# Small attention and third attention of a four-layer transformer chain: squares, root chains, key banks and transfers rearranged

## The chip, the cores and the metric

One Trainium2 chip, one core. The kernel is one program on that core. The metric is its device time in microseconds (us). Five engines have their own instruction streams and meet through semaphores: TensorE (PE), VectorE (DVE), ScalarE (ACT), GpSimd (POOL) and SyncE (SP, which issues the DMAs). SBUF is the large on-chip memory, PSUM the eight 2 KB-per-partition banks into which TensorE writes.

## What is computed

x is [8, 128, 512] in fp32 (8 batches of 128 tokens of 512 values). Eight stages follow, each of the form x = x + stage(layernorm(x)): attention with its own keys and bias (stage 0), a SiLU feed-forward with low-rank parts (1), the small attention (2), a feed-forward that picks one of 32 weights (3), the third attention, with normalised queries and keys (4), a mixture of low-rank experts (5), the last attention (6) and a GELU feed-forward (7). What bears on the change:

```python
# every stage: layernorm over the 512 values, mean and variance of each token

# small attention (stage 2): 8 batches x 4 patches of 128 positions, 8 heads of 8 values
scores = einsum('bhdi,bhdj->bhij', qh, kh) / sqrt(8)
scores = where(mask > 0, scores, -1e9);  attn = softmax(scores)
o = gelu(einsum('bhij,bhdj->bhdi', attn, vh))
out = (Wo @ o + bo) * mask

# third attention (stage 4): 32 query heads, 8 key/value heads, 128 values each
q = rmsnorm(q, q_norm_w);  k = rmsnorm(repeat(k, 4), k_norm_w)   # 1/sqrt(mean(square) + 1e-5)
attn = softmax(q @ k^T / sqrt(128) + mask);  out = (attn @ v) @ Wo
```

## The kernel before

**General.** Everything stays in SBUF: x (8 tiles of 128 x 512), the layernormed x transposed (xnT) and the context (ctxT), each as a high and a low part, so that an fp32 product is three matmul passes (`pe_matmuls`, L386). PSUM has eight banks: `proj[0..1]`, `score[0..1]`, `turn`, `heado`, `outp[0..1]`. The order on each engine is written out by hand; each engine runs its queue in that order, and a waiting instruction holds all behind it.

**Layernorm statistics.** Most stages get the mean from a sum that the last addition of the stage before delivers as it adds (`dve_add_sum`, L491), and the variance from squares with an accumulator on ScalarE (`act_ln_deviations`, L495). Stages 0 and 2 (`BN_STAGES`, L453) use two DVE instructions instead, `bn_stats` and `bn_aggr` (`dve_ln_stats`, L455, instructions at L457 and L459). Then `dve_ln_rstd` (L461) computes 1/sqrt for four batches at a time: one instruction for the argument (L466 or L468), two of bit tricks and three Newton steps of three instructions each (`dve_rsqrt`, L422, instructions L426 to L436), every one waiting for the one before; outside `BN_STAGES` one more for the shift (`recentre`, L473). Its arrays `nw_v`, `nw_t` and `rstd` lie in SBUF.

**Small attention** (L1733 to L2103). It follows the last output product of the SiLU feed-forward, whose eight additions to x are L1593. Head of the stage on DVE (`l1_dve`, from L2057): add and statistics for batches 0 to 3, adds 4 and 5, first root chain, normalised x of batches 0 and 1 (`norm`, L1988), masked keys of batch 0 (L1995), adds 6 and 7 with the other statistics, low part of the queries (L2000), values of batch 0 (L2009), last statistics, the second root chain, and only then the loop over 64 units (8 batches x 8). A unit is 4 heads of one patch: PE forms the scores (L1852) from a block-diagonal key tile, DVE takes the row maximum (L2016), ACT the exponentials (L1945), PE turns them (L1860) and multiplies with the values (L1872). Work for the next batch is strewn among the units of the present one (`extras`). POOL (`l1_pool`) makes the low part of the keys (L1799), the live mask of the *next* batch (`mask_keys`, L1789), and then the eight block-diagonal key tiles of the present batch (L1808), which also need rows of the mask that SP brings (`rows`, L1754, four small DMAs a batch). SP (`l1_sp`) waits for the last product of the feed-forward and issues one mask row for the tail (L1764), eight mask tiles for the tail (`tail`, L1745), and then `rows(0)`.

**Third attention** (L853 to L1310, `A.normed`). Eight groups g of one key/value head and four query heads j; a step (g, j) on PE is: scores of the next head, the projections that are `needed`, pieces of an output product (`out_at`), for each half a turn of the probabilities (L937) and a product with the values into `heado` (L950), then turns. For the root mean squares, raw queries and (at j = 1) the raw keys of the next group are turned by PE into `proj[0]` and `proj[1]` (`turn_for_sums`, L872, L883) and ScalarE squares and sums them from there (`sum_squares`, L1052, L1060). At j = 1 the queries come first, then the keys, into the same two banks. DVE makes the roots (`rms`, L1199, instructions L1207 and L426 to L436) with work values in `heado` (queries) or `score[0]` (keys). At j = 2 of every group but the last (`spreads`) DVE runs the keys' root chain, adds two output products to x (L1233), makes eight diagonals (`make_diagonals`, L1214), and PE spreads the roots over `turn` (L892). Group 0 and the last group are written out, groups 1 to 6 are a loop. PE's projection in a step waits for the squares of the last turns into `proj` (`last_sums`, L788).

## Time and profile before

| | us |
|---|---|
| median of 3 runs | 3076.47 (3075.88 to 3076.72) |
| profiled execution | 3081.03 |
| its span, first to last instruction | 3079.2 |
| PE busy | 2936.5 (95%) |
| DVE busy | 1723.2 (56%) |
| ACT busy | 1113.6 (36%) |
| POOL busy | 986.4 (32%) |
| small attention, first last-addition to next feed-forward | about 1108 to 1319 |
| third attention | about 1539 to 2216 |

Busy time is the sum of instructions; a PE at 95% still idles 143 us in the span, and it is there, at the joints between stages and in short waits inside a group, that a change of order can act. The chain of work that ended last runs through PE for 88% of the span and through DVE for 7%.

### The profile page before, as it was taken

What the parts mean: (1) busy time and instruction counts of PE and PEld (TensorE: products, weight loads), DVE (VectorE), ACT (ScalarE), POOL (GpSimd) and SP (SyncE); (2) the same over time, 40 slices, a digit from 0 to 9 for tenths busy, and PEclk for the clock granted to TensorE, in tenths of its full rate; (3) what the DMA queues carried; (4) which work ended last, traced back from release to release, by engine and by line L of the source; (5) the groups of instructions that cost most, each with busy time, mean ns of one, the idle gap of its engine ahead of it and who ended that gap; (6) DMA issues with size and microseconds to landing.
All of it is one profiled execution on the core that took longest, in us unless ns stands there. A gap on an engine that the chain in (4) does not pass through costs nothing.

```text
span 3079.2 us, 47940 instructions
## 1 busy us (share of the span) xinstructions
PE 2936.5 (95%) x16224; PEld 2492.1 (81%) x16224; DVE 1723.2 (56%) x3514; ACT 1113.6 (36%) x3615; POOL 986.4 (32%) x836
## 2 busy tenths in 40 slices
PE   7999999999999989899989999999889999999899
PEld 6888888888878857688778888888768888888787
DVE  6544444454552268777666666666644445444644
ACT  4222223222242237732344444444423333333432
POOL 4333333333222246433333222332213333332221
PEclk9999999999999999899999999999999999999999
DMA  3111101111111010011111001110011111110111
GB/s 120 41 48 40 47 30 47 39 40 47 37 49 48 27 42 29 27 35 41 32 39 32 28 27 34 34 34 17 25 41 41 39 37 34 34 34 21 45 45 48
DMA packets 68564, 119.74 MB, mean 39 GB/s; under 512 B 8681, under 2 KB 14185, under 8 KB 68065
## 3 DMA queue, kind: packets, MB, share of 16 engines
q1 hardware_dynamic: 68450, 118.26, 12.3%
q8 instruction: 67, 1.10, 0.1%
q14 instruction: 47, 0.39, 0.0%
HBM read 116.06 MB, written 2.10 MB: 38 GB/s over the span
## 4 chain that ended last, share of the span: by engine, by line
PE 88%; DVE 7%; ACT 3%; issue 2%; DMA 0%; POOL 0%; SPq 0%; DVEq 0%; ACTq 0%; POOLq 0%
PE proj L390 40%; PE outp L390 23%; PE heado L950 6%; PE score L917 5%; PE turn L937 3%; PE score L390 2%; PE outp L1872 1%; PE score L1454 1%; PE proj L406 1%; ACT sq L1060 1%; PE proj L883 1%; PE heado L1872 1%; DVE x L1691 0%; PE proj L1837 0%; PE turn L869 0%
## 5 line engine op out<-in xcount | busy, mean ns | idle before, releaser
L390 PE MATMUL outp<-w_out,acts 128*128 128x512 f32 x3288 | 840.7, 400 | 25.9 <-DVE x L1233 12.6
L390 PE MATMUL proj<-xnT,w_in 128*128 128x512 f32 x3192 | 758.0, 393 | 4.5 <-issue 2.3
L390 PEld LDWEIGHTS outp<-w_out,acts 128*128 128x128 f32 x3288 | 595.2, 188 | 154.0 <-DVE x L1233 16.4
L390 PEld LDWEIGHTS proj<-xnT,w_in 128*128 128x128 f32 x3192 | 593.6, 188 | 130.1 <-issue 2.7
L390 PE MATMUL proj<-ctxT,w_kv 128*128 128x512 f32 x1536 | 367.4, 395 | 18.7 <-POOL w_kv L697 18.7
L695 POOL TENSOR_TENSOR w_out<-ring,consts 128x512 fp32r<-128x512 f32 x96 | 101.9, 1062 | 830.0 <-PE outp L390 830.0
L390 PEld LDWEIGHTS proj<-ctxT,w_kv 128*128 128x128 f32 x1536 | 288.3, 190 | 77.8 <-issue 18.6
L1233 DVE TENSOR_TENSOR x<-x,outp 128x512 f32<-128x512 f32 x360 | 244.8, 685 | 186.7 <-PE outp L390 184.9
L1015 DVE COPY big<-proj 128x512 f32<-128x512 f32 x136 | 93.7, 689 | 348.7 <-PE proj L390 346.2
L1012 ACT ACTIVATE big<-proj 128x512 f32<-128x512 f32 x136 | 81.4, 599 | 496.9 <-PE proj L390 490.4
L695 POOL TENSOR_TENSOR w_kv<-ring,consts 128x512 fp32r<-128x512 f32 x93 | 97.0, 1043 | 459.6 <-DMA ring<-in_L_wk 439.3
L1093 ACT ACTIVATE acts<-heado 128x512 fp32r<-128x512 f32 x192 | 114.7, 597 | 325.1 <-PE heado L950 325.1
L1257 DVE TENSOR_TENSOR acts<-heado,acts 128x512 fp32r<-128x512 f32 x192 | 132.8, 692 | 174.1 <-ACT acts L1093 174.1
L950 PEld LDWEIGHTS heado<-ptbuf,big 128*128 128x128 f32 x1536 | 201.5, 192 | 30.9 <-ACT ptbuf L1091 15.6
L950 PE MATMUL heado<-ptbuf,big 128*128 128x128 f32 x1536 | 205.1, 277 | 12.3 <-ACT ptbuf L1091 6.9
L1091 ACT ACTIVATE ptbuf<-turn 128x512 f32<-128x512 f32 x192 | 114.3, 595 | 269.1 <-PE turn L937 268.8
L917 PEld LDWEIGHTS score<-big 128*128 128x128 f32 x1536 | 183.2, 192 | 8.9 <-issue 4.4
L917 PE MATMUL score<-big 128*128 128x128 f32 x1536 | 187.3, 275 | 3.0 <-issue 1.7
L390 PE MATMUL proj<-w_kv,ctxT 128*128 128x256 f32 x1536 | 183.4, 280 | 1.6 <-DVE big L1015 1.6
L390 PEld LDWEIGHTS proj<-w_kv,ctxT 128*128 128x128 f32 x1536 | 182.1, 188 | 3.1 <-DVE big L1015 1.9
L1593 DVE TENSOR_TENSOR x<-x,outp 128x512 f32<-128x512 f32 x160 | 109.7, 686 | 97.4 <-PE outp L390 97.0
L695 POOL TENSOR_TENSOR w_in<-ring,consts 128x512 fp32r<-128x512 f32 x96 | 106.6, 1111 | 166.1 <-PE proj L390 87.8
(303 smaller groups left out, 4129.3 us busy)
## 6 DMA issues: line engine op xcount, KB each, us to landing
ring<-in_L_wq SPq DMA_DIRECT2D x96, 256.0 KB, 2.7
ring<-in_L_wo SPq DMA_DIRECT2D x96, 256.0 KB, 2.6
ring<-in_F_in SPq DMA_DIRECT2D x52, 256.0 KB, 2.6
ring<-in_L_wk SPq DMA_DIRECT2D x48, 256.0 KB, 2.7
ring<-in_L_wv SPq DMA_DIRECT2D x48, 256.0 KB, 3.2
ring<-in_F_out SPq DMA_DIRECT2D x41, 256.0 KB, 2.6
x<-in_x SPq DMA_DIRECT2D x2, 1024.0 KB, 8.4
big<-in_ctxT SPq DMA_DIRECT2D x4, 512.0 KB, 8.0
```

Source lines behind the costliest of these rows:

```text
L390: mm = pe.matmul(bank_ap, w_ap(a, c), rhs(b, c), start=first and c == 0 and n == 0, stop=last and c == chunks - 1 and n == len(PASSES) - 1)
L695: pool.tensor_tensor(dst[:, slot, 0, :], ring[:, r, :], zeros512, ALU.add).then_inc(m["high_w"], 1)
L917: mm = pe.matmul(score[half][:, b * P:(b + 1) * P], qT[:, t], kT[:, t], start=True, stop=True)
L937: mm = pe.transpose(turn[:, b * P:(b + 1) * P], probs[j % 2][:, half, b * P:(b + 1) * P], ident)
L950: mm = pe.matmul(heado[:, b * P:(b + 1) * P], v_pair[:, n, j % 2, :] if A.own_kv else v[:, n * S:(n + 1) * S], ptbuf[:, half, b * P:(b + 1 ...
L1012: return engine.activation(dst, src, ACT.Copy)
L1015: return engine.tensor_copy(dst, src)
L1091: act.activation(ptbuf[:, half, :], turn[:, :], ACT.Copy).then_inc(m["tfree"], 1)
L1093: act.activation(acts[:, j, 0, half * HALF:(half + 1) * HALF], heado[:, :], ACT.Copy)\
L1233: dve.tensor_tensor(x[:, b, :], x[:, b, :], outp[b % 2][:, :], ALU.add).then_inc(m["added"], 1)
L1257: dve.tensor_tensor(acts[:, j, 1, cols], heado[:, :], acts[:, j, 0, cols].bitcast(F32), ALU.subtract)\
L1593: dve.tensor_tensor(x[:, b, :], x[:, b, :], outp[b % 2][:, :], ALU.add).then_inc(m["added"], 1)
```

## The change

Small attention: stage 2 leaves `BN_STAGES`; the feed-forward's last additions deliver sums; ScalarE squares; `norm` uses `rstd` and `recentre`. The second root chain goes from before the unit loop to behind unit 3, with its argument and work values in `outp[1]`. SP issues `rows(0)` ahead of the nine mask transfers. POOL makes the live mask of batch 1 after the second key tile, not before the first. Third attention: the raw keys at j = 1 are turned into `turn` and `heado`, with waits for those banks in place of the wait for the squares in `proj`; the query roots of that step work in `proj[1]`, so PE's next projection into `proj[1]` waits for the roots; the first addition of step j = 2 goes into the middle of the keys' root chain and the second behind it.

```diff
@@ dve_rsqrt
+        def dve_rsqrt(dve, y, arg, tmp, shifted, newton, calls, between=None):
...
             for n in range(3):
+                if n == 1 and between:
+                    between()
                 dve.tensor_tensor(tmp, y, arg, ALU.mult).then_inc(newton, 1)
...
-        BN_STAGES = [0, 2]
+        BN_STAGES = [0]
...
+        def dve_ln_rstd(dve, n, half, arg=None, work=None):
             cols = slice(half * BH, half * BH + BH)
+            arg, work = (nw_v[:, cols], nw_t[:, cols]) if arg is None else (arg, work)
...
+        def sum_banks(j, what):
+            return (turn, heado) if j == 1 and what == "k" else proj
...
         def last_sums(g, j):
-            return 5 * g + (2, 3, 4 if is_last_group(g) else 5, 6)[j]
+            return 5 * g + (2, 3, 4, 6)[j]
@@ project_head
                     m.wait(pe, "squared", 2 * squares + (half + 1))
+                if roots is not None and half == 1:
+                    m.wait(pe, "newton", 9 * roots)
@@ turn_for_sums
-                    m.wait(pe, "squared", 2 * c + (half - 1))
+                    if unit_left is None:
+                        m.wait(pe, "squared", 2 * c + (half - 1))
+                    elif half == 1:
+                        m.wait(pe, "low", unit_left + 1)
...
-                        mm = pe.transpose(proj[half][:, b * P:(b + 1) * P], src[:, t], ident)
+                        mm = pe.transpose(banks[half][:, b * P:(b + 1) * P], src[:, t], ident)
@@ attention_pe, step
-                    project(*new, squares=last_sums(g, j) if n == 0 else None)
+                    project(*new, squares=last_sums(g, j) if n == 0 else None,
+                            roots=newton_calls(g, j) if A.normed and j == 2 and n == 0 else None)
...
+                    if spreads(A, g, j) and half == 0:
+                        m.wait(pe, "squared", 2 * rms_call(g + 1, 0, "k") + 2)
                     m.wait(pe, "pready", unit(g, j, half) + 1)
@@ attention_dve, step
                 if spreads(A, g, j):
-                    rms(g + 1, 0, "k")
-                add_at(0)
+                    rms(g + 1, 0, "k", between=lambda: add(2 * out_g + pair, 0))
+                    add(2 * out_g + pair, 1)
+                else:
+                    add_at(0)
...
-                        rms(*n, lows=2 * (GH * g + j) + 2)
+                        rms(*n, lows=2 * (GH * g + j) + 2, scratch=proj[1] if j == 1 and not is_last_group(g) else None)
@@ ffn_dve, last_add
-                add(p, b, summed=A is F1)
+                add(p, b, summed=A is not F3)
@@ l1_sp
                     F0.events.wait(sp, "outfull", B * ((F0.chunks + 1) // 2))
+                    rows(0)
...
-                if b:
+                if b > 1:
                     rows(b - 1)
@@ l1_pool
-                if b + 1 < B:
+                if 0 < b < B - 1:
                     mask_keys(b + 1)
...
                 for u in range(UNITS):
+                    if b == 0 and u == 2:
+                        mask_keys(1)
@@ l1_act
+            for b in range(BH + 2):
+                deviations(b)
             F0.events.wait(act, "outfull", B * ((F0.chunks + 1) // 2))
...
+            for b in range(BH + 2, B):
+                deviations(b)
+            act.wait_ge(ln_moments, 8 * 2 + B)
             for u in range(UNITS * B):
@@ l1_dve
-            for b in range(BH):
+            for b in range(BH + 2):
                 add_of(b)
-                dve_ln_stats(dve, 2, b)
-            add_of(BH)
-            add_of(BH + 1)
             dve_ln_rstd(dve, 2, 0)
             norm(0)
             norm(1)
-            dve_ln_stats(dve, 2, BH)
             for s in range(2):
                 take_keys(0, s)
             add_of(BH + 2)
-            dve_ln_stats(dve, 2, BH + 1)
-            dve_ln_stats(dve, 2, BH + 2)
-            add_of(BH + 3)
             for s in range(2):
                 low_of_queries(0, s)
+            add_of(BH + 3)
             take_values(0)
-            dve_ln_stats(dve, 2, BH + 3)
-            dve_ln_rstd(dve, 2, 1)
             for u in range(UNITS * B):
                 maxima(u)
                 if u >= 2 and u % 2:
                     take_turned(u - 2)
                 extras(u // UNITS, u % UNITS)
+                if u == 3:
+                    dve_ln_rstd(dve, 2, 1, outp[1][:, 0:BH], outp[1][:, BH:B])
```

## Rows read from the trace of the kernel before

**Rows 1.** The page: busy time, share of the span, instructions of PE.

```profile
PE 2936.5 (95%) x16224; PEld 2492.1 (81%) x16224; DVE 1723.2 (56%) x3514; ACT 1113.6 (36%) x3615; POOL 986.4 (32%) x836
```

**Rows 2.** Windows: start:end, length, busy (instructions) per engine, granted clock, DMA, GB/s.

```profile
1128.00:1138.00 10.00, 4.59 (x6) 1.62 (x6) 9.55 (x16) 1.06 (x4) 7.18 (x8) 0.67 0.14 48
...
1158.00:1178.00 20.00, 18.43 (x126) 14.57 (x125) 17.61 (x28) 14.26 (x44) 12.24 (x11) 1.00 0.09 27
```

**Rows 3.** Timeline, DVE, small attention's head: start us, us, instruction [idle before, releaser].

```profile
1114.31 1.39 DVE L1593 TENSOR_TENSOR x<-x,outp 128x512 f32<-128x512 f32 x2
...
1128.18 1.04 DVE L466 TENSOR_SCALAR nw_v<-moments 128x4 f32<-128x4 f32 x1
...
1136.21 0.69 DVE L2016 TENSOR_REDUCE negmax<-score 128x4 f32<-128x512 f32 x1
...
1145.08 0.69 DVE L2016 TENSOR_REDUCE negmax<-score 128x4 f32<-128x512 f32 x1 [0.44 <-PE score L1852]
```

**Rows 4.** Timeline, PE, the same stretch.

```profile
1108.59 0.39 PE L1440 MATMUL outp<-low_b,low_in 96*128 96x512 f32 x1
...
1109.71 0.39 PE L1440 MATMUL outp<-low_b,low_in 96*128 96x512 f32 x1
...
1118.81 1.93 PE L1832 MATMUL proj<-sq,wk 128*96 128x512 f32 x4 [1.66 <-DVE sq L1988]
...
1128.46 0.77 PE L1852 MATMUL score<-stacks 98*128 98x512 f32 x1 [1.77 <-POOL stacks L1808]
...
1138.22 0.77 PE L1852 MATMUL score<-stacks 98*128 98x512 f32 x1 [5.18 <-ACT pbuf L1945]
```

**Rows 5.** Timeline, POOL, the same stretch.

```profile
1124.10 1.48 POOL L1789 TENSOR_SCALAR brow<-ring 96x512 f32<-96x512 f32 x1
1127.16 8.02 POOL L1808 TENSOR_TENSOR stacks<-spare,consts 98x512 fp32r<-98x512 f32 x8 [1.58 <-DMA spare<-ring]
```

**Rows 6.** Timeline, SP's DMA issues, the same stretch.

```profile
1117.19 0.24 SPq L1764 DMA_DIRECT2D big<-in_mask  x1
...
1122.62 2.48 SPq L1754 DMA_DIRECT2D spare<-ring  x4
```

**Rows 7.** Timeline, ACT: a table load in this head; another, with what follows.

```profile
1123.42 1.28 ACT L1945 ACT_TABLE_LOAD   x1
...
1283.04 1.28 ACT L1978 ACT_TABLE_LOAD   x1
1284.34 1.95 ACT L1978 ACTIVATE big<-big,vecs 64x512 f32<-64x512 f32 x3
```

**Rows 8.** Timeline, PE, third attention, j = 1 to j = 2 of one group.

```profile
1764.32 0.66 PE L883 MATMUL proj<-consts,spare 128*128 128x128 f32 x4 [0.85 <-ACT sq L1060]
1765.35 0.66 PE L883 MATMUL proj<-consts,spare 128*128 128x128 f32 x4 [0.37 <-ACT sq L1060]
...
1777.44 1.67 PE L390 MATMUL outp<-w_out,acts 128*128 128x512 f32 x6 [0.86 <-DVE x L1233]
...
1781.67 1.05 PE L950 MATMUL heado<-ptbuf,big 128*128 128x128 f32 x8
```

**Rows 9.** Timeline, DVE, the same group.

```profile
1763.27 0.69 DVE L1257 TENSOR_TENSOR acts<-heado,acts 128x512 fp32r<-128x512 f32 x1 [0.83 <-ACT acts L1093]
...
1766.20 0.16 DVE L1207 TENSOR_SCALAR heado<-sumsq 128x8 f32<-128x8 f32 x1
...
1773.45 0.69 DVE L1015 COPY big<-proj 128x512 f32<-128x512 f32 x1 [1.08 <-PE proj L390]
...
1776.70 1.29 DVE L1233 TENSOR_TENSOR x<-x,outp 128x512 f32<-128x512 f32 x2 [0.23 <-DVE rk L436]
1777.90 1.65 DVE L1214 TENSOR_SCALAR spare<-consts,rk 128x128 f32<-128x128 f32 x8
...
1780.67 0.69 DVE L1257 TENSOR_TENSOR acts<-heado,acts 128x512 fp32r<-128x512 f32 x1 [0.52 <-ACT acts L1093]
```

**Rows 10.** Timeline, POOL, the same group.

```profile
1765.81 1.60 POOL L697 TENSOR_TENSOR w_in<-ring,w_in 128x512 fp32r<-128x512 f32 x1
```

More of the change, by code:

```diff
@@ L459, in dve_ln_stats @@
             dve.bn_aggr(moments[:, b, :], stats[:, b, :]).then_inc(ln_moments, 1)
-        def dve_ln_rstd(dve, n, half):
+        def dve_ln_rstd(dve, n, half, arg=None, work=None):
             cols = slice(half * BH, half * BH + BH)
+            arg, work = (nw_v[:, cols], nw_t[:, cols]) if arg is None else (arg, work)
             dve.wait_ge(ln_moments, 8 * n + half * BH + BH)
             if n in BN_STAGES:
-                dve.tensor_scalar(nw_v[:, cols], moments[:, cols, 1], EPS, None, ALU.add).then_inc(ln_rstd, 1)
+                dve.tensor_scalar(arg, moments[:, cols, 1], EPS, None, ALU.add).then_inc(ln_rstd, 1)
             else:
-                dve.tensor_scalar(nw_v[:, cols], sqdev[:, cols], 1.0 / D ** 3, EPS, ALU.mult, ALU.add).then_inc(ln_rstd, 1)
+                dve.tensor_scalar(arg, sqdev[:, cols], 1.0 / D ** 3, EPS, ALU.mult, ALU.add).then_inc(ln_rstd, 1)
             dve.wait_ge(ln_rstd, 2 * n + half + 1)
-            dve_rsqrt(dve, rstd[:, cols], nw_v[:, cols], nw_t[:, cols], ln_shifted, ln_newton, ln_calls[0])
+            dve_rsqrt(dve, rstd[:, cols], arg, work, ln_shifted, ln_newton, ln_calls[0])
             ln_calls[0] += 1
@@ L476, in centred @@
         def centred(n, half):
-            return 7 + 2 * (ln_no(n) - 1) + half + 1
+            return 7 + 2 * (n - 1) + half + 1
         NORMED_DVE = (4, 6)
@@ L830, in project_values, with project_head @@
                 mm.then_inc(m["pfull", half], 1)
-        def project_head(pe, A, g, j, what, squares=None, halves=(0, 1)):
+        def project_head(pe, A, g, j, what, squares=None, roots=None, halves=(0, 1)):
             m = A.events
@@ L855, in attention_pe @@
             unit = lambda g, j, half: 2 * (GH * g + j) + half
-            project = lambda g, j, what, squares=None: project_head(pe, A, g, j, what, squares)
+            project = lambda g, j, what, squares=None, roots=None: project_head(pe, A, g, j, what, squares, roots)
             def use_turn(n):
@@ L870, in turn_values, with turn_for_sums @@
                 mm.then_inc(m["tfull"], 1)
-            def turn_for_sums(g, j, what, taken):
+            def turn_for_sums(g, j, what, taken, banks=proj, unit_left=None):
                 c = rms_call(g, j, what)
@@ L957, in step @@
                 for new in turned_for_sums(A, g, j):
-                    turn_for_sums(*new, taken=needed(A, g, j)[-1])
+                    banks = sum_banks(j, new[2])
+                    turn_for_sums(*new, taken=needed(A, g, j)[-1], banks=banks,
+                                  unit_left=None if banks is proj else unit(g, j, 1))
                 if spreads(A, g, j):
@@ L1050, in attention_act, with sum_squares @@
             m = A.events
-            def sum_squares(g, j, what):
+            def sum_squares(g, j, what, banks=proj):
                 c = rms_call(g, j, what)
@@ L1059, in sum_squares @@
                         n = half * BH + b
-                        a = act.activation(sq[:, n * P:(n + 1) * P], proj[half][:, b * P:(b + 1) * P], ACT.Square,
+                        a = act.activation(sq[:, n * P:(n + 1) * P], banks[half][:, b * P:(b + 1) * P], ACT.Square,
                                            accum_out=sumsq[:, n:n + 1])
@@ L1097, in step @@
                 for new in turned_for_sums(A, g, j):
-                    sum_squares(*new)
+                    sum_squares(*new, banks=sum_banks(j, new[2]))
             def group(g):
@@ L1197, in normalise, with rms @@
                    .then_inc(m["pready"], 1)
-            def rms(g, j, what, lows=0):
+            def rms(g, j, what, lows=0, scratch=None, between=None):
                 m.wait(dve, "low", lows)
@@ L1204, in rms @@
                 m.wait(dve, "squared", 2 * c + 2)
-                scratch = score[0] if what == "k" else heado
+                scratch = scratch or (score[0] if what == "k" else heado)
                 mean, work = scratch[:, 0:B], scratch[:, B:2 * B]
@@ L1208, in rms @@
                 m.wait(dve, "meaned", c + 1)
-                dve_rsqrt(dve, dst[:, :], mean, work, m["shifted"], m["newton"], c)
+                dve_rsqrt(dve, dst[:, :], mean, work, m["shifted"], m["newton"], c, between)
             def make_diagonals():
@@ L1927, in l1_act, with deviations @@
             act.wait_ge(m["w_made"], 3)
+            def deviations(b):
+                F0.events.wait(act, "added", B * ((F0.chunks - 1) // 2) + b + 1)
+                act_ln_deviations(act, 2, b)
             def high_of_keys(b, s):
@@ L1987, in norm @@
                 wait(dve, m["q_full"], 2 * b - 2)
-                dve.tensor_scalar(xn1[b % 2], x[:, b, :], moments[:, b, 0:1], rstd[:, b:b + 1], ALU.subtract, ALU.mult)\
+                dve.wait_ge(ln_rms, centred(2, b // BH))
+                dve.tensor_scalar(xn1[b % 2], x[:, b, :], rstd[:, b:b + 1], recentre[:, b:b + 1], ALU.mult, ALU.add)\
                    .then_inc(m["normed"], 1)
```

3 lines of the change are left out of this document (1 added, 2 removed).

## The prediction

> **What bounds the kernel now.** I read the page first: PE is busy for 95% of the span [rows 1], so an edit pays where PE idles, or where PE runs at its lower clock, and nowhere else. Then the list of waits and PE's timeline in the two stages that the diff touches, and for every PE gap the timelines of the engines behind it.
>
> In the small attention's head PE all but stops. From 1128 to 1138 us it is busy 4.59 of 10 us, at a mean granted clock of 0.67 (one level is 2.4 GHz, the other, half of it, 1.2 GHz), while DVE is busy 9.55 us [rows 2]. The reader is to see why: the first scores are there at 1128.46 [rows 4], but DVE takes their maximum only at 1136.21, because the second root chain stands ahead of it from 1128.18 [rows 3]. That chain is 12 tiny instructions in 8.0 us, the first of 1.04 us; beside it POOL makes key tiles, eight in 8.02 us [rows 5]. In the third attention the same chain of 12 takes 2.4 us: from the end of the copy at 1773.45 + 0.6 to the add at 1776.70, less 0.23 of wait [rows 9], so 0.20 us each. Once the units run, PE is busy 18.43 of 20 us at full clock [rows 2]: a later start is never made up, and an earlier one is kept.
>
> In the third attention the gaps come once in each of seven groups (all but the last): 0.85 and 0.37 us ahead of the turned keys, which wait for ScalarE to empty `proj`, and 0.86 us ahead of an output product that waits for DVE's addition [rows 8]. They sum to 2.1 us of modelled idle time; from start to start the rows lose up to 2.4.
>
> **Small attention, step by step.** *Additions and statistics.* Six additions, four statistics and the chain stand ahead of the first norm. They end at 1114.31 + 1.39 = 1115.7 [rows 3]. Without the statistics PE sets the pace: two products in a row close 1.12 us apart [rows 4], an addition takes 0.7 [rows 3]. Product 2 closes at 1110.1, its addition begins at 1110.2, three more at 1.1 bring the sixth to 1113.5 and its end to 1114.2: 1.4 us earlier. The read of the accumulator that a summing add brings has 0.4 us of room in each step, so I cost it at nothing; without that room it would add under 0.1 us a step by my guess from the 0.16 to 0.2 us of the smallest instructions [rows 9], at most 0.6 in all. The chain gets one instruction more (`recentre`, 0.2). ScalarE, idle there, squares the first four batches beside it. Norm, PE's key projection (1118.81, released by the norm [rows 4]) and all behind it come 1.2 us earlier.
>
> *Rows first.* SP issues the row transfers at 1122.62, 5.4 us after its wait ended at 1117.19 [rows 6], and POOL starts the key tiles at 1127.16, having idled 1.58 us for them [rows 5]. Put first, they are issued over 2.5 us from about 1115.7 and land before 1121; nothing waits for them. What is late next is POOL's own queue: the low part of the keys ends where the mask begins, 1124.10 [rows 5], now 1122.9. The nine mask transfers move 2.5 us back in SP's queue; their reader is the stage's tail, over 100 us later. `ctx_tok` of batch 2 is queued behind them, and it needs values of batch 1, later still.
>
> *Live mask of batch 1.* It goes behind two key tiles. So POOL does tiles 0 and 1 (2.0 us) until 1124.9, the mask (1.5) until 1126.4, tile 2. DVE's masked keys of batch 1 (unit 0's extra) wait for that mask, and the maximum of unit 1 is queued behind them: about 1.5 us of DVE wait, which I count. From a tile's start to its scores is 1.3 us (1127.16 to 1128.46 [rows 4, 5]). Unit 2's scores, at 1138.22 before [rows 4], come at 1126.4 + 1.3 = 1127.7: **10.5 us earlier**.
>
> *Table load.* The load for the exponentials ran at 1123.42, long before the first of them [rows 7]. Squares of batches 6 and 7 now stand ahead of it; the last ends near 1124.5, the load 1.3 later at 1125.8, the first exponentials at 1127.0. That is under the 1127.7 that POOL sets, so it costs nothing. The Trainium skill (ScalarE: Activation LUTs, What ACT_TABLE_LOAD costs) speaks against this: it counts a drain of some 1.4 us on top of the load, 2.7 in all, which would push unit 2 to about 1128.4 and cost 0.7 us. The trace does not agree: 1.30 us from a load's start to the next instruction's [rows 7].
>
> *The late chain.* 13 instructions, behind unit 3. At 0.20 us each they hold DVE 2.6 us; DVE idled 0.44 there before the maximum of unit 4 at 1145.08 [rows 3]. Behind it wait low queries, then PE's value projection, then every later unit: 2.2 us lost on the path. POOL is multiplying beside it. With work values in SBUF each could cost 1.0 as in the 8.0 us above; with them in PSUM, the chain at 1766.20 ran in 0.2 steps (first instruction 0.16 us [rows 9]) beside a POOL instruction of 1.60 us [rows 10]. Only `recentre` still reads two SBUF arrays: up to 0.8 more. I take 2.4, near the row that has PSUM. The Trainium skill (GPSIMD Engine Reference, Specifications) says that POOL contends with DVE instructions in a two-port mode or with two SBUF inputs; by this rule the last instruction alone is exposed, and the rows agree.
>
> Sum for the stage: 10.5 - 2.4 = **8.1 us**, bounds 5 (late chain 3.0, additions and mask worse by 2) and 11 (PE not falling to its half clock, which now costs some 2.6 us of the work behind 1138).
>
> **Third attention, step by step.** *Banks.* The first half of the keys goes to `turn`, free at once; the second to `heado`, free when DVE's low part of 1763.27 ends, 1764.0 [rows 9], instead of 1765.35 [rows 8]: PE reaches its scores 1.35 us earlier. The squares of the keys stay where they are on ScalarE: their gate is DVE's read at 1766.20 [rows 9].
>
> *New waits.* PE's projection into `proj[1]` waits for the query roots, 1766.20 + 12 x 0.2 = 1768.6 [rows 9]. PE is there at 1764.5 + 1.7 + 2.8 = 1769.0, so it costs nothing, with 0.4 us of room; behind this wait stand output products, turns, everything of the step. The wait on `turn` for the keys' squares (over by 1768.7) is met long before.
>
> *Addition inside the chain.* DVE was free at 1773.45 - 1.08 = 1772.4 and waited for PE [rows 9]; the projection now ends at 1771.8, so DVE starts at 1772.4. Copy 0.6, six of twelve root instructions 1.2: the first addition runs from 1774.2 to 1775.0, and the product of 1777.44 [rows 8] can start 2.4 us earlier. But what is late next is DVE: six more (1.2), second addition (0.6), diagonals (1.6), third addition (0.6), with 0.4 of small waits, sum from 1772.4: 0.6 + 2.4 + 1.8 + 1.6 + 0.4 = 6.8, so the low part of 1780.67 [rows 9] starts at 1779.2, ends at 1779.8, and PE's second `heado` product starts at 1779.9 rather than 1781.67 [rows 8]. That is **1.8 us a group**, times 7 = **12.6 us**. Bounds: 1.0 (DVE shifts only by the 1.08 us that it idled) and 2.4 (DVE keeps up), so 7 to 17 us.
>
> **Sum.** 8.1 + 12.6 = 20.7 us. The profiled execution took 3081.0 us (its span 3079.2), 4.5 above the median of the runs; from its own time 3060.3, from the median 3076.5 - 20.7 = **3055.8 us**. About 0.2% (6 us) is what a measurement can tell from no change.
>
> **Rivals.**
> - *DVE is the bound.* If DVE's queue of the step moves only by what it idled, the third attention gives 1.0 a group: 3076.5 - 8.1 - 7.0 = 3061.4. For: it is back to back for 6 us there. Against: the sum of its pieces. 0.13.
> - *The late chain is still held up by POOL.* 13 x 1.0 - 0.4 = 12.6 us lost instead of 2.4, so the small attention gains nothing (2.1 worse): 3066.0. Against: rows 9 and 10. 0.08.
> - *The edits of the third attention do nothing*, since squares, not banks, gate PE: 3068.4. Against: the product of 1777.44 names DVE's addition. 0.04.
> - *Slower: PE waits for the query roots.* The root chain runs while POOL splits weights [rows 10]. If each of its 12 instructions took 1.0 us, the roots would be ready at 1778.2, 7.7 us after PE's old start in `proj[1]` (1770.5); times 7, less 8.1: 3122. It decides as soon as the chain ends after 1772.5, 0.33 us more per instruction, for slower by 6 us. Against: the same chain, in the same place, in another bank, is not held up. 0.04.
> - Nothing measurable for other reasons, 0.03. The forecast, 0.68.
>
> Its own range is 3048.5 to 3064.5; reaching to the second rival gives **3048 to 3067**. Faster 0.93 (forecast and first three rivals), within 0.2% 0.03, slower 0.04.
>
> **What would show it.** Right: unit 2's scores near 1127.7, without the 5 us PE gap ahead of them; 13 instructions of 0.2 us behind unit 3; no PE wait on `sq` L1060 in front of keys; a short or no wait of the product for the addition; groups of the third attention 1.8 us shorter. Wrong: a PE wait in front of the `proj[1]` projection on `rq`; a PE wait in front of the second `heado` product longer than 0.6 us; root instructions of 1 us; the first exponentials waiting for the table load; PE's half clock lasting longer than before.

## The result, and the profile after

The changed kernel took **3060.26 us** (median of 4 runs, 3059.8 to 3064.65) against 3076.59 for the kernel before beside it: ratio 0.995, 95% interval 0.9938 to 0.9962. It is faster by 16.3 us, where the prediction said 20.7 and 3055.8 us. Its profiled execution has a span of 3062.8 us, 16.4 less than the 3079.2 of before.

I cut both spans at moments that PE passes in both kernels, each one row of PE's timeline, and subtract (us):

| segment | before | after | difference |
|---|---|---|---|
| start to the feed-forward's product 0 (L1440, now L1459) | 1107.56 | 1109.19 | +1.63 |
| to the value projection of batch 7, small attention | 152.24 | 142.93 | **-9.31** |
| to the first scores of the next feed-forward | 59.85 | 60.62 | +0.77 |
| to the last products of that feed-forward | 189.28 | 192.41 | **+3.13** |
| to the third attention's first projection | 32.56 | 33.73 | **+1.17** |
| third attention | 673.99 | 663.00 | **-10.99** |
| rest | 863.72 | 860.92 | -2.80 |

The first and the last line hold the same instructions in both kernels; they differ by executions. The third attention's line is not free of this either: with the same code in the stage it took 660.81 (third_only), 660.56 (rows_last), 662.22 (early_load) and 663.00 us (after), while the groups inside it agree within 0.1 us.

**Head of the small attention.** PE's timeline of after (start us, us, instruction, idle before and its releaser), key projection and then unit 2's scores; it answers to [rows 4]:

```profile
1109.19 0.49 PE L1459 MATMUL outp<-low_b,low_in 96*128 96x512 f32 x1 [1.33 <-DVE low_in L1683]
...
1118.93 2.91 PE L1854 MATMUL proj<-sq,wk 128*96 128x512 f32 x4 [2.06 <-DVE sq L2020]
...
1130.29 0.47 PE L1874 MATMUL score<-stacks 98*128 98x512 f32 x1 [0.95 <-ACT pbuf L1971]
...
1138.45 1.08 PE L1866 MATMUL proj<-biasbuf,ring 128*128 128x64 f32 x8 [1.59 <-DVE stacks L2032]
```

From product 0 to unit 2's scores it is 21.10 us; before it was 30.66 (1138.22 - 1107.56). The wait of 5.18 us is gone. The windows (PE busy is the first number behind the length, the granted clock the third from the end) show PE 7.57 of 10 us busy at full clock where [rows 2] had 4.59 at 0.67:

```profile
1128.00:1138.00 10.00, 7.57 (x40) 4.74 (x38) 7.33 (x21) 7.83 (x23) 9.75 (x10) 1.00 0.13 37
```

DVE, of after; the last addition ahead of the first root chain, the late chain's first and last instruction and the maximum behind it; it answers to [rows 3]:

```profile
1114.93 0.69 DVE L496 SCALAR_TENSOR_TENSOR x<-outp,x 128x512 f32<-128x512 f32 x1 [0.29 <-PE outp L1459]
...
1134.22 0.15 DVE L471 TENSOR_SCALAR outp<-sqdev 128x4 f32<-128x4 f32 x1
...
1136.61 0.31 DVE L476 SCALAR_TENSOR_TENSOR recentre<-sumx,rstd 128x4 f32<-128x4 f32 x1
1136.85 0.68 DVE L2048 TENSOR_REDUCE negmax<-score 128x4 f32<-128x512 f32 x1
```

The chain in PSUM holds DVE from 1134.22 to 1136.85, 2.6 us for 13 instructions, beside a busy POOL. SP issues the rows first, POOL starts its tiles without idle time and puts the mask behind two of them; ScalarE loads its table only when the maximum is there (DVE's L2048, over at 1127.63). SP, POOL, ACT; they answer to [rows 5 to 7]:

```profile
1116.97 2.53 SPq L1773 DMA_DIRECT2D spare<-ring  x4
```
```profile
1124.71 2.04 POOL L1830 TENSOR_TENSOR stacks<-spare,consts 98x512 fp32r<-98x512 f32 x2
1126.71 1.49 POOL L1809 TENSOR_SCALAR brow<-ring 96x512 f32<-96x512 f32 x1
1128.28 6.03 POOL L1830 TENSOR_TENSOR stacks<-spare,consts 98x512 fp32r<-98x512 f32 x6
```
```profile
1127.71 1.28 ACT L1971 ACT_TABLE_LOAD   x1 [0.35 <-DVE negmax L2048]
1129.00 2.18 ACT L1971 ACTIVATE pbuf<-score,negmax 128x128 f32<-128x128 f32 x8
```

**Third attention.** PE's waits over about one group (1640 to 1722 us; columns: waited for, us in total, times, longest), first of before, then of after:

```profile
PE proj L883 <- ACT sq L1060: 1.2, 2, 0.8
PE outp L390 <- DVE x L1233: 0.9, 1, 0.9
PE turn L892 <- DVE big L1222: 0.3, 1, 0.3
```
```profile
PE heado L965 <- DVE acts L1276: 0.5, 1, 0.5
PE turn L904 <- DVE big L1239: 0.3, 1, 0.3
```

The waits of [rows 8] are gone and a shorter one has come, ahead of the second product with the values. A group, from one set of diagonals (L1214, now L1231) to the next, takes 83.18 us before and 81.51 after. DVE's timeline of after shows the first addition behind the first of the chain's three Newton steps, and from the second addition on a queue without a gap, which answers to [rows 9]:

```profile
1768.03 0.69 DVE L1250 TENSOR_TENSOR x<-x,outp 128x512 f32<-128x512 f32 x1 [0.23 <-DVE rk L438]
...
1770.03 0.69 DVE L1250 TENSOR_TENSOR x<-x,outp 128x512 f32<-128x512 f32 x1 [0.21 <-DVE rk L438]
1770.64 1.65 DVE L1231 TENSOR_SCALAR spare<-consts,rk 128x128 f32<-128x128 f32 x8
1772.21 0.68 DVE L1250 TENSOR_TENSOR x<-x,outp 128x512 f32<-128x512 f32 x1
1772.81 0.68 DVE L1276 TENSOR_TENSOR acts<-heado,acts 128x512 fp32r<-128x512 f32 x1
```

**Where gain was lost.** The next feed-forward starts at half clock in this execution. PE's timeline of before and of after, its first scores and first projections there:

```profile
1319.65 2.02 PE L1454 MATMUL score<-factors,big 16*128 16x128 f32 x16 [0.73 <-issue]
1321.60 5.74 PE L390 MATMUL proj<-xnT,w_in 128*128 128x512 f32 x24
```
```profile
1312.74 2.32 PE L1473 MATMUL score<-factors,big 16*128 16x128 f32 x16 [0.73 <-issue]
1315.00 8.59 PE L390 MATMUL proj<-xnT,w_in 128*128 128x512 f32 x24
```

The granted clock (third from the end) of the windows says the same: it had come back, and fell again. Before, then after:

```profile
1322.00:1327.00 5.00, 5.00 (x24) 4.12 (x23) 4.89 (x7) 0.60 (x1) 3.93 (x3) 1.00 0.00 0
```
```profile
1310.00:1315.00 5.00, 4.27 (x26) 3.38 (x25) 1.06 (x2) 1.11 (x2) 0.00 (x0) 0.93 0.00 0
1315.00:1320.00 5.00, 5.00 (x13) 3.94 (x13) 4.89 (x7) 0.00 (x0) 3.88 (x3) 0.50 0.00 0
```

### The profile page after: what moved, and what is told of

Same layout as the page of the kernel before. It is cut to its first block, busy times and chain, and to the rows that moved or that the text cites. A ratio compares the mean times of both kernels' runs of the same rounds, so it can differ in the third digit from the quotient of the medians.

```text
span 3062.8 us, 47964 instructions
## 1 busy us (share of the span) xinstructions
PE 2935.8 (96%) x16224; PEld 2493.0 (81%) x16224; DVE 1709.6 (56%) x3508; ACT 1122.2 (37%) x3631; POOL 986.7 (32%) x836
## 4 chain that ended last, share of the span: by engine, by line
PE 86%; DVE 8%; issue 3%; ACT 3%; POOL 1%; DMA 0%; DVEq 0%; SPq 0%; POOLq 0%; ACTq 0%
PE proj L390 39%; PE outp L390 23%; PE heado L965 6%; PE score L929 5%; PE turn L952 2%; PE score L390 2%; PE score L1473 1%; PE outp L1894 1%; PE proj L406 1%; DVE pbuf L1189 1%; DVE acts L1276 1%; PE heado L1894 1%; ACT acts L1110 1%; DVE x L1710 0%; PE proj L895 0%
## 5 line engine op out<-in xcount | busy, mean ns | idle before, releaser
L1276 DVE TENSOR_TENSOR acts<-heado,acts 128x512 fp32r<-128x512 f32 x192 | 132.7, 691 | 174.3 <-ACT acts L1110 174.3
```

The source lines that it names most:

```text
L1276: dve.tensor_tensor(acts[:, j, 1, cols], heado[:, :], acts[:, j, 0, cols].bitcast(F32), ALU.subtract)\
```

## The experiments

Ratios with an interval are to the kernel before on the same chip. Where one execution is given, it is the profiled one, and its whole time is worth little: four of after_again span 2.6 us, ten of low_first 18.

**The two halves.** *small_only*: the third attention as before, the small attention as changed. *third_only*: the reverse.

```diff
 small_only
-            return (turn, heado) if j == 1 and what == "k" else proj
+            return proj
...
-                    rms(g + 1, 0, "k", between=lambda: add(2 * out_g + pair, 0))
-                    add(2 * out_g + pair, 1)
+                    rms(g + 1, 0, "k")
+                add_at(0)
...
 third_only
-        BN_STAGES = [0]
+        BN_STAGES = [0, 2]
...
-                if u == 3:
-                    dve_ln_rstd(dve, 2, 1, outp[1][:, 0:BH], outp[1][:, BH:B])
...
```

> Only the small attention's part is left in; the third attention is as before. Theory A: the units of the small attention start 9.3 us earlier, counted from the feed-forward's last product, and what the whole kernel gains is that less or more what PE's clock level at the joints makes of it: 5 to 9 us faster than before. Theory B: the gain in the units is really lost in the next feed-forward, because the earlier start meets something late there: under 4 us faster. Theory C: the parts add up to less than each alone (DVE or POOL coupled between stages): 9 us or more alone.

> Only the third attention's part is left in; the small attention is as before. Theory A: seven groups 1.6 us shorter each, 11.2 us faster, PE's second product into heado waits about 0.5 us in every group for DVE's low part. Theory B: the three waits of before all go, 2.3 us a group, 16 us faster, and the changed kernel lost the rest elsewhere. Theory C: 7 us, DVE moving only by the 1.08 us that it had idled.

Measured: small_only 3072.94 us (12 runs; before beside it 3081.4), ratio 0.9977 (0.9967 to 0.9986), so 4 to 10 us. third_only 3065.96 (5 runs), ratio 0.9956 (0.9943 to 0.9969), so 10 to 18 us. The profile of small_only has the stage's gain (value projection of batch 7 142.98 us behind product 0) and the losses behind it (192.39 and 33.75 us); that of third_only has neither (189.26 and 32.60), and its group takes 81.53 us, its third attention 660.81, 13.2 less than before. The two gains add to that of the whole (0.0023 + 0.0044 against 0.0063 in after_again), and the small attention is the half that yields less than it gains in its own stage.

**The same kernel again.** *after_again* is the changed kernel once more, to see whether the half clock was that one execution's.

> The changed kernel itself, profiled once more. Theory A: the half clock over the first 24 matmuls of the feed-forward behind the small attention (8.59 us instead of 5.74) belongs to that execution; here it is at another joint or missing, and the joints differ by 1 to 4 us while the groups of the third attention are the same to 0.1 us. Theory B: the half clock there belongs to the change: again 8.6 us at that place.

Measured: 3059.66 us, ratio 0.9937 (0.9922 to 0.9952), and 192.40 and 33.68 us again. I then took the half clock for a property of the change; further down a run takes that back.

**PSUM for the late chain.** *chain_sbuf* gives the chain behind unit 3 its old arrays in SBUF.

```diff
-                    dve_ln_rstd(dve, 2, 1, outp[1][:, 0:BH], outp[1][:, BH:B])
+                    dve_ln_rstd(dve, 2, 1)
```

> The changed kernel with the late root chain's argument and work values back in SBUF (nw_v, nw_t); its place behind unit 3 stays. Theory A (POOL and DVE contend over SBUF): the instructions of the chain that run beside a POOL instruction take about 1.0 us instead of 0.17, the chain takes 5 to 8 us instead of 2.7, and PE's wait ahead of the value projection of batch 1 grows by as much from 1.6 us. Theory B (PSUM is not what helps, the place is): the chain stays at 2.6 us.

Measured in one execution (3064.76 us): the chain takes 6.8 us instead of 2.6, PE's wait ahead of the value projection is 5.73 instead of 1.59, and the value projection of batch 7 comes 147.74 us behind product 0 instead of 142.93. DVE's timeline of chain_sbuf, and POOL's beside it:

```profile
1131.14 0.54 DVE L471 TENSOR_SCALAR nw_v<-sqdev 128x4 f32<-128x4 f32 x1
1131.71 0.17 DVE L426 TENSOR_SCALAR nw_t<-nw_v 128x4 int32<-128x4 int32 x1
1131.91 1.14 DVE L428 TENSOR_SCALAR rstd<-nw_t 128x4 int32<-128x4 int32 x1
1133.09 1.20 DVE L434 TENSOR_TENSOR nw_t<-rstd,nw_v 128x4 f32<-128x4 f32 x1
...
1135.41 0.16 DVE L438 SCALAR_TENSOR_TENSOR rstd<-nw_t,rstd 128x4 f32<-128x4 f32 x1
...
1136.00 0.99 DVE L438 SCALAR_TENSOR_TENSOR rstd<-nw_t,rstd 128x4 f32<-128x4 f32 x1
1137.02 0.96 DVE L476 SCALAR_TENSOR_TENSOR recentre<-sumx,rstd 128x4 f32<-128x4 f32 x1
```
```profile
1131.73 2.54 POOL L1819 TENSOR_TENSOR spare<-maskadd,spare 32x512 fp32r<-32x512 f32 x2
1134.36 1.48 POOL L1809 TENSOR_SCALAR brow<-ring 96x512 f32<-96x512 f32 x1
1135.93 6.03 POOL L1830 TENSOR_TENSOR stacks<-spare,consts 98x512 fp32r<-98x512 f32 x6
```

The bank is what keeps the chain short. The reader is to see more. Beside POOL's TENSOR_TENSOR (two inputs in SBUF) a small instruction lasts until the POOL instruction that was running at its start is over: L428 ends at 1133.06 and L434 at 1134.29, POOL's at 1133.03 and 1134.27. The seven long ones of before (from 1128.18, [rows 3]) end 0.02 us behind POOL's key tiles in the same way. So the price of one is what is left of POOL's instruction. Beside POOL's one-input TENSOR_SCALAR (1134.36 to 1135.84) five took 0.16 us and one 0.46.

**The chain in pieces.** *split_chain* issues the same 13 instructions in four pieces, behind units 1 and 2 and within units 3 and 5; *split_timed* is the same kernel, timed on another chip.

```diff
+        def late_chain(dve, part):
...
                 maxima(u)
+                if u in (3, 5):
+                    late_chain(dve, u // 2 + 1)
                 if u >= 2 and u % 2:
                     take_turned(u - 2)
                 extras(u // UNITS, u % UNITS)
-                if u == 3:
-                    dve_ln_rstd(dve, 2, 1, outp[1][:, 0:BH], outp[1][:, BH:B])
+                if u in (1, 2):
+                    late_chain(dve, u - 1)
```

> The changed kernel with the late root chain cut into four pieces, one each behind unit 1, behind unit 2, and ahead of the turned copies of units 3 and 5, where DVE idled 0.5 to 0.9 us. Theory A (the chain of 13 instructions in one piece is what PE waits for ahead of the value projection of batch 1): that wait of 1.6 us goes to under 0.5, the value projection comes 1.3 us or more earlier, counted from the last product of the feed-forward (29.3 us now). Theory B (something else, POOL or ScalarE, would be late there anyway): 29.3 again.

> The late chain in four pieces between the units, timed. Theory A (the pieces hide in DVE's idle time, and the next feed-forward starts at full clock in most executions): median near 3051 us, ratio to before 0.991 to 0.993; segments 6.7 us from unit 2 to the value projection, 189.3 and 32.7 for the next feed-forward and the joint behind it. Theory B (the full clock in the one look was chance): median 3056 to 3059, ratio 0.9935 to 0.995, and the profiled execution shows 192.4 and 33.7 again.

Measured: 3050.41 us in one execution; timed 3049.86 (5 runs, 3049.29 to 3053.83), **ratio 0.9908 (0.9895 to 0.992)**. PE's wait ahead of the value projection is gone, and the next feed-forward starts at full clock in both profiles. PE of split_chain:

```profile
1132.07 1.08 PE L1892 MATMUL proj<-biasbuf,ring 128*128 128x64 f32 x8
```
```profile
1307.00:1312.00 5.00, 5.00 (x23) 4.06 (x23) 4.86 (x8) 0.60 (x1) 3.92 (x3) 1.00 0.00 0
```

From product 0 to the value projection of batch 1 it is 27.78 us (after 29.26), of batch 7 140.92 (142.93): 2.0 us are the order itself. The next feed-forward (189.24) and the joint behind it (32.66) are those of before: another 4.2. split_timed is close but not the same: 28.51, 141.65, 190.35 and 32.33, with half clock in 1496.4 to 1499.8, near the end of the feed-forward. That the pieces are what brings the full clock back is not shown; see the last experiment.

**Is it the joint's short gaps?** *warm_joint* adds 14 products of 256 columns into a free bank ahead of the small attention's eight output products.

```diff
+            def fill(count):
...
             def out_product(b):
+                fill((2, 1, 1, 1, 1, 1, 1, 6)[b])
```

> The changed kernel with small extra products of constants on PE, into a free bank, in the gaps of the small attention's tail, 14 in all, most of them in the 5.1 us gap ahead of the last output product. They do nothing for the result. Theory A (PE's half clock from there to the first 24 matmuls of the next feed-forward, 8.59 us instead of 5.74, comes from how little PE has to do in that tail): the clock is up in the tail, the 24 matmuls take 5.7 us, and the kernel is 4 to 8 us faster. Theory B (the level does not hang on it, or the extra products hold up the real ones as much as they give): within 1.5 us.

Measured: 3058.5 us (8 runs, 3054.69 to 3069.44), ratio 0.9945 (0.9927 to 0.9962), which overlaps that of after_again; from the last value projection to the next feed-forward 60.58 us, then 192.43 and 33.72. PE kept full clock longer in the joint (to 1291, where after_again fell at 1281), fell after it all the same, and the feed-forward started at half clock as in after. The added work bought nothing that these runs can show.

**The table load.** *early_load* lets ScalarE issue a one-column exponential, and so the load, ahead of the squares of batches 6 and 7.

```diff
+            act.activation(sumsq[:, 0:1], consts[:, C_ONES:C_ONES + 1], ACT.Exp)
             for b in range(BH + 2, B):
                 deviations(b)
```

> The changed kernel with one tiny exponential on ScalarE ahead of the squares of batches 6 and 7, so that the table load stands there and not behind the wait for the first maximum. Theory A (the load is exposed: it starts 0.35 us after the maximum and the exponentials follow it): unit 2's scores no longer wait 0.95 us for the exponentials and come 0.5 to 0.95 us earlier, counted from the last product of the feed-forward (21.1 us now). Theory B: POOL's live mask sets unit 2, under 0.2 us.

Measured in one execution (3059.47 us): the exponentials no longer wait for a load, but unit 2's scores come 21.15 us after product 0, as in after_again. ACT and PE of early_load:

```profile
1122.27 1.28 ACT L1998 ACT_TABLE_LOAD   x1
...
1125.21 1.14 ACT L1971 ACTIVATE pbuf<-score,negmax 128x128 f32<-128x128 f32 x4
```
```profile
1125.43 1.42 PE L1874 MATMUL score<-stacks 98*128 98x512 f32 x1
1126.65 1.50 PE L1854 MATMUL proj<-sq,wk 128*96 128x512 f32 x2
1127.57 0.81 PE L1874 MATMUL score<-stacks 98*128 98x512 f32 x1
```

Unit 2's scores have no wait in front of them here: PE is at half clock in this place (two key projections 1.99 us, where after took 1.07) and is itself what is late. after_again has the same half clock and, with its load behind the maximum, no wait there either, so at this clock the load's place is worth nothing. What it costs when PE has its full clock there is bounded by the wait of 0.95 us in after, and was not isolated.

**The rows first.** *rows_last* puts `rows(0)` back behind the nine mask transfers.

```diff
-                    rows(0)
                     sp.dma_start(flat[E1:E1 + 1, :], ...)
...
-                if b > 1:
+                if b:
                     rows(b - 1)
```

> One part undone: SP again issues the first batch's mask rows behind the nine mask transfers of the tail. Theory A (the rows were on the path, POOL sets the units' start): POOL's key tiles start some 2.2 us later, with a POOL idle time ahead of them that names the DMA; unit 2's scores come 23.3 us after the feed-forward's last product instead of 21.15, and the value projection of batch 1 near 31.5 instead of 29.3. Theory B (the start is set by DVE's queue and the table load ahead of the first exponentials): unit 2's scores move by less than 0.8 us. For the clock at the start of the next feed-forward (half in every run with a late chain in one piece, full before and with the chain in pieces): if the level hangs on the moment at which the stage comes, a shift of 2 us may bring the full clock back (189.3 us from its first scores to its last products, 192.4 at half clock); if it hangs on the one-piece chain, it stays 192.4.

Measured in one execution: POOL idles for the DMA again,

```profile
1125.29 2.04 POOL L1829 TENSOR_TENSOR stacks<-spare,consts 98x512 fp32r<-98x512 f32 x2 [1.54 <-DMA spare<-ring]
```

and starts 16.89 us after product 0 instead of 15.52. Unit 2 comes 0.9 us later (22.04), the value projection of batch 1 1.4, that of batch 7 2.1. So the rows are on the path, for about half of what I expected at unit 2. The next feed-forward took 191.97 us, neither of the two lengths that I had named. Its whole time (3071.43) is no price of this part: the first 30 us behind the third attention ran at a granted clock of 0.54 in this execution, and that rest took 870.3 us, 9.4 more than in after.

**The order in the third attention.** *low_first* puts the low part (L1276) ahead of the third addition in the step j = 2; *add_behind* puts the first addition back behind the whole root chain; *split_low* is low_first together with the chain in pieces.

```diff
 low_first
                 for half in range(2):
-                    add_at(1 + half)
+                    late = spreads(A, g, j) and half == 0
+                    if not late:
+                        add_at(1 + half)
...
                        .then_inc(m["low"], 1)
+                    if late:
+                        add_at(1 + half)
 add_behind
-                    rms(g + 1, 0, "k", between=lambda: add(2 * out_g + pair, 0))
-                    add(2 * out_g + pair, 1)
-                else:
-                    add_at(0)
+                    rms(g + 1, 0, "k")
+                add_at(0)
```

> The changed kernel with one edit in the third attention: at j = 2 DVE takes the low part of heado's first half ahead of the third addition, not behind it. Theory A (DVE's queue is the bound behind the diagonals, as the sum of its pieces said): the wait of 0.48 us ahead of PE's second heado product goes in all seven groups, each group is 0.4 to 0.5 us shorter, 3.3 us in all. Theory B (the low part waits for ScalarE or PE, not for DVE's queue): nothing changes.

> One part undone: the first addition of the third attention's step j = 2 goes back behind all twelve root instructions. Theory A (the addition inside the chain is what lets the output product start early): a wait of that product for the addition comes back, 0.3 to 0.9 us, and each of the seven groups is 0.5 to 1.0 us longer: the stage takes 666.5 to 670 us instead of 663.0. Theory B (DVE's whole queue is the bound of the step, whatever the order inside it, and the gain came from the banks): the stage stays within 1 us of 663.0, since the wait ahead of the second product with the values is the same.

> The late chain in pieces, and in the third attention the low part ahead of the third addition. Theory A (the two gains add, and the longer rest of the kernel seen with the low part first was that execution's clock): the third attention takes 657 us, the rest as in the run beside it, median 3044 to 3047, ratio 0.989 to 0.991. Theory B (the shorter third attention brings stages behind it to half clock each time): third attention 657 us, but the rest 872 us instead of 858 to 861, median 3054 to 3060, no better than with the pieces alone.

Measured, from diagonals to diagonals (six periods in each profile, alike within 0.1 us but for the first of low_first and of split_low, 81.25): before 83.18, add_behind 82.02, after 81.51, low_first and split_low 80.90 us a group. add_behind took 3057.49 us in its one execution, its third attention 665.89 us, a little under the 666.5 of its theory A. In add_behind the wait for the addition is back:

```profile
1762.56 1.66 PE L390 MATMUL outp<-w_out,acts 128*128 128x512 f32 x6 [1.15 <-DVE x L1250]
```

In low_first the wait ahead of the second product with the values is gone:

```profile
1766.55 1.13 PE L965 MATMUL heado<-ptbuf,big 128*128 128x128 f32 x8
```

Of the 1.67 us a group, 1.16 come with the banks alone and 0.5 with the addition inside the chain on top of them (the addition with the old banks was not run); that last wait is worth 0.6 more. The times do not follow it safely: low_first 3062.38 us (10 runs from 3053.37 to 3071.73), ratio 0.9946 (0.993 to 0.9962); split_low 3053.56 (3045.73 to 3063.3), ratio 0.9917 (0.9899 to 0.9935). In the profiled execution of low_first the third attention is 6.1 us shorter than in after (seven groups of 0.6 are 4.3 of it), and the rest of the kernel 12 us longer, most of it right behind the stage, where PE has full clock in after and mostly half in low_first. After, then low_first:

```profile
2202.00:2232.00 30.00, 24.15 (x159) 20.03 (x160) 21.38 (x51) 6.80 (x15) 0.00 (x0) 1.00 0.03 8
```
```profile
2191.00:2221.00 30.00, 28.55 (x129) 27.36 (x130) 12.64 (x34) 6.42 (x12) 0.00 (x0) 0.54 0.00 1
```

split_low's profiled execution did not have this (0.93 in the same place). Its third attention took 657.9 us and its rest 862.8, and its median lies between its two theories. Its six times, 18 us apart, and low_first's ten go with a level that changes from one execution to the next; only one of each was profiled. I would keep the chain in pieces without low_first: the two intervals overlap, and the five times of split_timed lie within 5 us.

**The half clock once more.** rows_last and add_behind have the late chain in one piece, add_behind with not one instruction of the small attention changed. Both ran on another chip than after_again and the runs made beside it, and both show 5.74 us for the 24 projections at the start of the feed-forward: full clock. add_behind:

```profile
1308.39 2.02 PE L1471 MATMUL score<-factors,big 16*128 16x128 f32 x16 [0.73 <-issue]
1310.34 5.74 PE L390 MATMUL proj<-xnT,w_in 128*128 128x512 f32 x24
```

The whole segment (first scores to last products) says more than its start. With the late chain elsewhere or in pieces it took 189.28 (before), 189.26 (third_only), 189.24 (split_chain), 189.27 (split_low) and 190.35 us (split_timed). With the chain in one piece it took 192.4 (after, after_again, small_only, chain_sbuf, warm_joint), 193.5 (early_load, low_first), 191.97 in rows_last, where the clock fell at 1334 instead of at the start, and 190.34 in add_behind, which kept full clock from the start to 1495. In small_only and early_load the 24 projections took 7.0 us, half clock for a part of them. So one of nine profiled executions with the chain in one piece is as short as the longest of the others. That the chain in one piece causes the loss every time is refuted; that it makes it likely fits, with one execution each and the chip changed along with the order. On the second chip alone the pieces are worth little: from product 0 to the third attention it is 426.57 us in add_behind and 424.24 in split_timed, 2.3 us, where the first chip has 430.03 in after_again and 422.80 in split_chain, 7.2 us.

## Why the prediction came out as it did

The sign and the range were right; the forecast was 4.5 us too low. That distance is hardly safe: the interval of the first measurement (0.9938 to 0.9962) ends short of the 20.7 us that I forecast (0.9933), the one of after_again (0.9922 to 0.9952) holds it. What the pieces gave is safer, from rows.

- **Additions, statistics, norm.** Right. The sums pace at 1.0 us, the key projection comes 9.74 us behind product 0 instead of 11.25: 1.5 against 1.2.
- **Late chain.** Right: 2.6 us of DVE for 13 instructions, `recentre` 0.31. On the path it cost 2.0 us, by split_chain at batch 7 (1.6 between add_behind and split_timed), against 2.4. The rival in which POOL holds it up is what chain_sbuf shows without the PSUM bank. The Trainium skill (GPSIMD Engine Reference, Specifications) has this contention as a rule for DVE's two-port modes and two SBUF inputs. The trace agrees for two inputs (1.20 us for L434 beside two-input work on POOL); L428, with one input, took 1.14 us there, and no run shows its port mode. The time with PSUM work values beside the same POOL work is 0.17.
- **Rows first.** Right in kind; at unit 2 it was worth 0.9 us (rows_last), where I had expected 2.2 when I undid it.
- **Live mask.** I counted 1.5 us of DVE wait. DVE's key instruction at 1128.29 had [0.66 <-PE proj L1854] in front of it; the mask ended at 1128.2, in the same moment as PE's projection, so at most those 0.66 us are its.
- **Unit 2 and the table load.** Wrong by 0.96 us: unit 2's scores come 9.56 us earlier, not 10.5, and the wait in front of them (0.95 us) is for ScalarE, not for POOL's tile. I had compared the *start* of the first exponentials (19.4 us behind product 0) with the scores that POOL's tile allows (20.1). Unit 2's scores wait for their end: 1129.00 to 1130.29 is 1.29 us, and 1.28 in before (1136.94 to 1138.22). Adding it gives 20.7, 0.6 of the miss; the rest is that the exponentials came 0.37 us later than forecast, as the load stood behind DVE's maximum (0.35 us of idle time). In before it had not: it ran at 1123.42 [rows 7], the maximum came at 1136.21 [rows 3]. Nor does the third attention's load in after:

```profile
1550.68 1.28 ACT L1089 ACT_TABLE_LOAD   x1
1555.13 0.40 ACT L1089 ACTIVATE tbuf<-tbuf,negmax 128x128 f32<-128x128 f32 x1 [3.17 <-DVE negmax L1195]
```

  What differs is the code in front: the changed kernel puts a second wait (`act.wait_ge(ln_moments, ...)`, L2000) directly ahead of the wait for the maximum (L1968). In the trace of after the maximum's wait is then an instruction of its own, at 1127.7, with the load behind it; in before it belongs to the first exponential, behind the load. That the second wait is the cause is my reading of the two traces; no run took it out.
- **Sum of the stage.** 10.5 at unit 2 less 2.4 was the forecast; measured to the last value projection 9.3. That it is not below the 8.1 is luck: unit 2 was 0.96 short, and the chain cost about what I said, but PE's clock gave back 1.8 us that stood in my upper bound and not in the sum. In before PE ran at half clock behind unit 2's scores, in after at full, and from unit 2's scores to unit 5's it is 7.91 us before and 6.09 after. Before:

```profile
1138.22:1143.00 4.78, 4.78 (x10) 2.57 (x11) 1.98 (x3) 2.97 (x10) 1.28 (x1) 0.50 0.01 2
```

- **The step that failed**: "an earlier one is kept". It was kept through the units only. The segments behind them cost 0.8 + 3.1 + 1.2 = 5.1 us, so that 4.2 arrive at the third attention. The prediction named "PE's half clock lasting longer than before" as what would show it wrong, and gave it no price and no place a stage further on. Why the clock falls there stays open.
- **Third attention.** Mechanism right: the bound passes to DVE's queue, seen as a wait of 0.48 us ahead of the second product with the values. 1.67 us a group against 1.8. The bound of 1.0 that takes only what DVE idled is near the 1.16 of the banks alone; my 1.8 had the addition in it, worth 0.5. The stage gave 10.99 instead of 12.6: six periods 10.05, the stage's start 1.4, its end -0.45. In third_only the same code gave 13.18 (six periods 9.9, the start 2.4, the end 0.9), so the stage's ends move by some 2 us between executions, and what the groups show is the safer number: 0.13 us short of the forecast in each.
- **Slower rival** (PE waits for the query roots). The roots ran from 1759.95 to 1762.3 in `proj[1]`, 0.2 us apiece, over before PE needed the bank; no wait on `rq`.

In the one pair of profiles, the forecast missed by the joints: 5.1 us of clock and waits behind the small attention and 1.6 in the third attention, against 1.2 gained over the forecast in the units; the rest differs by executions (+1.63 and -2.80 in the table).

## What to carry to other kernels

A small DVE instruction with its operands in SBUF that must run beside POOL's two-input work lasts until POOL's instruction is over; a row of dependent ones pays that each time. Give it PSUM operands, and if it still stands ahead of something that PE needs, cut it into pieces small enough for the gaps between the maxima. Here the pieces gave 2.0 us by their order (1.6 on the other chip). The medians stand 10 us apart (3049.86 in split_timed, 3059.66 in after_again, on different chips); the rest goes with the clock level and the executions, and the runs do not show that the pieces cause it. Take a gain of a stage to the start of the next two stages before counting it, by the length of segments between the same instructions: at a joint where PE is at half clock for a while, a few us may be given back. When a step waits for another engine's result, compare the end of that engine's work, not its start. And when a wait is added in front of an activation that needs another table, see in the trace on which side of the load the wait for its data stands.

## What the runs showed of the hardware that I had not expected

- The granted clock can fall in one execution and not in another at a place that the same code leads up to: 24 projections took 5.74 us in add_behind and 8.59 us in after and low_first, with 60.4 to 60.6 us from the last value projection to the feed-forward's first scores in all three.
- 14 filler products ahead of that place kept the clock up for some 10 us and changed nothing behind (192.43 against 192.41 us).
- A table load can run long before its activation's data is there (1123.42, 12.2 us of idle time behind it, in before), and it can stand behind the wait for that data (1127.71 in after). Either way it takes 1.29 to 1.30 us from its start to the next instruction's when that one has nothing to wait for.
- POOL's TENSOR_TENSOR stretches DVE instructions of 4 columns in SBUF from 0.16 to 1.0 to 1.2 us, until its own end; beside its TENSOR_SCALAR with one input five of six took 0.16 us in chain_sbuf.
